# A decoder layer on one core: all mixer tiles at one pace of four steps, weights split one piece a step

## What is computed

```
x = _layernorm(x + mixer(x))            # state-space mixer over chunks of 64, 4 heads, with gate and RMS norm
x = _layernorm(x + xattn(x, ctx, ctx))  # 16 heads of 8, softmax over 256 keys
x = _layernorm(x + ffn(x))              # 8 experts, top 2 of them, 128 -> 512 -> 128, silu
```

## Time and profile before

| | |
|---|---|
| median of 3 runs | 405.66 us (405.43 to 405.94) |
| the profiled execution | 404.54 us, span 403.2 us |
| TensorE busy | 347.0 us (86%) |
| VectorE busy | 258.6 us (64%) |
| ScalarE busy | 220.2 us (55%) |
| POOL busy | 203.8 us (51%) |
| DMA | 41.97 MB, mean 104 GB/s |
| first maxima, exponentials of step 0 and of step 63 | 76.2, 107.5 and 260.1 us |

### The profile page before, as it was taken

One profiled execution on the slowest core, in us unless ns is written; L12 is line 12 of the kernel. 1 busy time (PEld: TensorE's weight loads), 2 busy tenths in 40 slices (PEclk: granted clock), 3 DMA queues, 4 the chain that ended last, 5 costly groups with the idle time before them and its releaser, 6 DMA issues.

```text
span 403.2 us, 8839 instructions
## 1 busy us (share of the span) xinstructions
PE 347.0 (86%) x2869; PEld 237.9 (59%) x2869; DVE 258.6 (64%) x794; ACT 220.2 (55%) x413; POOL 203.8 (51%) x297
## 2 busy tenths in 40 slices
PE   1999877889898999988888899989999999999900
PEld 0666654556543546454444455568878989999800
DVE  3555646788888888888888836466564444343427
ACT  2677645523476666656567776643545555555304
POOL 2760588865453535163648586535464332323425
PEclk9999999999999999999999999999999999999965
DMA  8933222545425122050723544211123211111054
GB/s 269 353 103 98 90 93 65 184 134 170 139 64 154 46 84 67 16 161 3 243 91 104 170 125 134 61 40 48 53 60 90 68 39 55 41 52 43 27 189 138
DMA packets 44461, 41.97 MB, mean 104 GB/s; under 512 B 4560, under 2 KB 38416, under 8 KB 44416
## 3 DMA queue, kind: packets, MB, share of 16 engines
q1 hardware_dynamic: 41136, 35.10, 29.0%
q0 software_dynamic: 2272, 4.69, 3.3%
q10 hardware_dynamic: 1008, 1.61, 1.1%
HBM read 26.36 MB, written 14.75 MB: 102 GB/s over the span
## 4 chain that ended last, share of the span: by engine, by line
PE 58%; DVE 18%; POOL 9%; issue 9%; ACT 4%; DMA 2%; ACTq 0%; POOLq 0%; DVEq 0%
PE banks L1028 13%; PE banks L1053 8%; DVE nm L1217 7%; PE banks L870 4%; PE banks L1043 4%; PE banks L709 4%; PE banks L918 3%; PE banks L766 2%; PE banks L774 2%; DVE ctx_in L1159 1%; PE banks L929 1%; PE banks L948 1%; PE banks L861 1%; POOL cs_wide L1616 1%; PE banks L817 1%
## 5 line engine op out<-in xcount | busy, mean ns | idle before, releaser
L1217 DVE TENSOR_REDUCE nm<-banks 128x4 f32<-128x1024 f32 x64 | 78.1, 1220 | 13.7 <-PE banks L861 12.8
L1517 ACT ACTIVATE probs_all<-banks 128x1024 f32<-128x1024 f32 x64 | 65.5, 1023 | 38.5 <-PE banks L870 38.3
L1702 POOL DMA_INDIRECT y_dram<-x,scatter_u x39 | 37.5, 962 | 55.4 <-DVE x L1364 53.1
L1028 PE MATMUL banks<-w_split,scores_in 128*128 x234 | 64.1, 409 | 0.0
L1349 DVE TENSOR_TENSOR ctx_in<-ctx_in,banks 128x512 f32<-128x512 f32 x39 | 26.8, 687 | 58.0 <-ACT ctx_in L1559 58.0
L1028 PEld LDWEIGHTS banks<-w_split,scores_in 128*128 128x128 f32 x234 | 40.8, 189 | 7.5 <-issue 0.7
L1691 POOL DMA_INDIRECT slots_dram<-rows,place_u x32 | 31.7, 991 | 25.0 <-DVE count L1309 17.6
L1559 ACT ACTIVATE ctx_in<-banks 128x512 f32<-128x512 f32 x39 | 23.3, 597 | 35.2 <-PE banks L1028 35.2
L1053 PEld LDWEIGHTS banks<-w_down,hsT 128*128 128x128 f32 x312 | 39.9, 191 | 3.2 <-issue 0.6
L1053 PE MATMUL banks<-w_down,hsT 128*128 x312 | 41.4, 276 | 0.2 <-DVE scores_in L1354 0.2
L870 PE MATMUL banks<-scores_in 32*128 32x256 f32 x256 | 32.2, 326 | 9.9 <-DVE nm L1217 5.2
(11 more groups left out here) (224 smaller groups left out, 701.4 us busy)
## 6 DMA issues: line engine op xcount, KB each, us to landing
scores_in<-k_dram SPq DMA_DIRECT2D x32, 128.0 KB, 2.6
scores_in<-q_dram SPq DMA_DIRECT2D x32, 128.0 KB, 2.7
ctx_in<-in_L_ffn_w SPq DMA_DIRECT2D x16, 256.0 KB, 3.4
cs_wide<-cs_dram SPq DMA_DIRECT2D x14, 256.0 KB, 3.6
scores_in<-slots_dram SPq DMA_DIRECT2D x39, 65.0 KB, 1.9
k_dram<-split_qk SPq DMA_DIRECT2D x8, 256.0 KB, 2.5
q_dram<-split_qk SPq DMA_DIRECT2D x8, 256.0 KB, 2.3
w_down<-in_L_ffn_wo SPq DMA_DIRECT2D x8, 256.0 KB, 3.5
```

The costliest lines, as they stand in the source:

```text
L1028: m = TE.matmul(up_bank(i, j), xT[:, i % XT, xh, :], all_up[:, c + j * FF:][:, bass.ds(expert_at[i] * UP_ALL, FF)], start=n == 0, stop=n == 2)
L1217: V.tensor_reduce(most, maxima_of(n).rearrange("p (j k q) -> p j k q", j=2, k=TPS), AX_X, ALU.max, negate=True).then_inc(s["nmax"], 1)
L1517: C.activation(probs(n).rearrange("p j k q -> p (j k q)"), EXPS, ACT.Exp, scale=SCALE).then_inc(s["probs"], 1)
L1702: G.indirect_dma_start(y_dram[:, :], bass.IndirectOffsetOnAxis(ap=scatter_u[:, i:i + 1], axis=0), y_slot[:, i % Y_RING, :], None).then_inc ...
```

## The change

Three things go together. `tile_step` becomes 4t - 33 for all tiles: tile 1 stands one step later than before, tile 7 and all behind it seven steps, and `LAST_MIXER` goes from 32 to 39. What is counted from it moves along: the second slot for maxima (from step 41), the first loads of weights (43) and the first split (45). From there on each step splits one piece, up to step 60, and every other one also loads down weights. The fillers in the mixer's bank move by three steps, so that they follow it, and `second_slot` and the wait of `scores` are written for the new parity.

```
-FIRST_TILES, FIRST_PACE, PACE = 7, 3, 4
+PACE = 4
...
-UNREAD_IN_MIX = {1: S, 4: S, 5: P, 8: 3 * P, 9: S, 13: 3 * P, 16: 3 * P, 17: 3 * P, 21: S, 24: 3 * P}
+UNREAD_IN_MIX = {4: S, 7: S, 8: P, 11: 3 * P, 12: S, 16: 3 * P, 19: 3 * P, 20: 3 * P, 24: S, 27: 3 * P}
...
 def tile_step(t):
-    return FIRST_PACE * min(t, FIRST_TILES) + PACE * max(t - FIRST_TILES, 0) - LEADS_IN
+    return PACE * t - LEADS_IN
...
-        elif n >= LAST_MIXER + 6 and piece + whole_pieces < PIECES + NE:
-            if (n - LAST_MIXER) % 3 == 2:
+        elif n >= LAST_MIXER + 6 and piece < PIECES:
+            yield "split_weights", piece
+            if W_RING <= piece + 2 < PIECES:
+                yield "load_weights", piece + 2
+            if piece % 2:
                 yield "load_down", whole_pieces
                 whole_pieces += 1
-            else:
-                yield "split_weights", piece
-                if W_RING <= piece + 2 < PIECES:
-                    yield "load_weights", piece + 2
-                piece += 1
+            piece += 1
...
         def second_slot(n):
-            return n - LEAD > LAST_MIXER and (n - LEAD - LAST_MIXER) % 2 == 1
+            return n - LEAD > LAST_MIXER and n % 2 == 0
...
-                    slots = 2 if later - LEAD > LAST_MIXER else 1
+                    slots = 2 if later - 1 - LEAD > LAST_MIXER or second_slot(later) else 1
```

## The result

| | before | changed |
|---|---|---|
| median of four runs | 405.55 us (405.40 to 405.94) | 423.54 us (420.10 to 428.35) |
| profiled execution, its span | 404.54, 403.2 us | 424.87, 423.6 us |
| mean granted clock of TensorE over the span | 0.980 | 0.921 in the profiled run, 0.911 to 0.943 in the others |

The ratio is 1.0386, with a 95% interval of 1.0332 to 1.044: slower, by 18 us between the medians where 4.9 were forecast. The ratio leaves out the run of 428.35 us, taken in a slower state, and comes to some 16 us. The time lies above the forecast's range. Where the four runs of the kernel before stay within 0.6 us of each other, those of the changed one spread over 8, and the granted clock differs along with them.

A forecast was written before the change was run, and what follows sets the result against it. It took batch 0's queries to bound the lead-in, and a nearly full TensorE the later stretches. -1.2 + 2.2 + 0.6 + 2.6 - 0.8 + 1.5 = +4.9 us on 405.66 gave 410.6 us, range 405.2 to 414.2.

The forecast's parts named there:

- rival 4: TensorE's clock falls in the gap ahead of the first maxima: +3 us, so 413.6 us; chance 0.02.
- A: Lead-in: fewer operations beside batch 0's query chain bring the first maxima earlier, -1.2 us (+0.2 to -2.5).
- D: Roots of batches 6 and 7 queue behind scatters on POOL, steps 26 and 34: +2.6 us (0.5 to 3.5).
- B: Behind the first maxima: more mixer work for TensorE and VectorE, +2.2 us (0 to 3.2).
- E: Full eight steps of attention and mixer: heavier steps spread, TensorE's gaps partly given back, -0.8 us (0 to -2.7).
- C: Second slot for maxima opens at step 41, not 33: light steps between get longer, +0.6 us (0 to 1.2).
- F: Weight loads through a ring of four places: ScalarE waits for landings at pieces 7 and 15, +1.5 us (0 to 4).
- Rival 1: Tiles, not the queries, pace the lead-in: fewer tiles save 6.8 rather than 1.2 us, 404.2 us; chance 0.10.
- Rival 2: All of the change is absorbed by gaps and TensorE's other work: +0.1 us, 405.8 us; chance 0.08.
- Rival 3: The weights' ring becomes the bound, ScalarE waits at several pieces: 5 us there, 414.1 us in all; chance 0.12.

The follow-up runs named there:

- roots_first: The changed kernel with the scatters of batches 0 and 1 behind the roots of steps 26 and 34, plus lead-in fillers: 413.85 us, ratio 1.0143.
- roots_weights: roots_first with no split of weights in steps 49 and 50: 410.98 us, ratio 1.0067 to the kernel before.
- weights_only: The kernel before with only the change's part on the weights, the mixer's pace untouched: 418.99 us, ratio 1.0016.
- lead_41: The changed kernel with a lead-in of 41 steps instead of 33 and weights split from step 37 on: 435.73 us, ratio 1.0427 to the kernel before.
- before_late_rows: The kernel before with the scatters of batch 0's rows in step 27, not 24: 422.65 us, ratio 1.0102.

## Why the prediction was wrong

The direction was right and the size was not: +4.9 forecast, +18 measured. By its own steps:

- **The step that failed is the likelihood and the price of rival 4, the fall of the clock.** I gave it 0.02 and 3 us, for one fall in the wait for the queries, directly ahead of the first maxima. In the profile TensorE has no wait there at all. The gap stood 12.5 us earlier, in the wait for x1 of batch 0, which the sum of part A doesn't have; that its 3.08 us match the 2 or 3 foreseen is luck. And the clock fell three more times, and TensorE's later stretches, where it is the bound, paid for it: 12.8 of 20.4 us between the profiles. My "some 3 us of work" took only what stands right behind the gap. A stretch of 17.1 us at 1.2 GHz cost 6.4 us and another 5.6. The Trainium skill's rule (TensorE: Matmul & The Clock Gate, section "What's actually happening") is that the gate closes after idleness and opens again after sustained work. The first half agrees with the changed kernel's trace, in that each fall came in or shortly behind waits, though of 0.8 to 3.1 us only; the second half does not, with 16.93 of 17.1 us of work at 1.2 GHz from 213.6. I had the rule and read it as a remark on one spot instead of asking it of each wait that steps A and D added.
- **A, lead-in, -1.2.** In the changed kernel the queries' last load was issued at 72.3 us, 73.0 before, with a landing of 3.1 us at most, and TensorE, at half clock up to 73.7, took them up only at 76.98. With the lead-in's fillers it does wait for the queries, 1.0 to 2.1 us, as A said, and in roots_first the first reduction came at 76.0, 0.9 before the old 76.9; in the three other runs with fillers at 77.0 to 77.6. Right in kind, but the gain was 0.9 at best; x1 of batch 0 came only 0.2 us earlier. Tile 1's gate took 0.72 for 1.67 as hoped, while the norm of two tiles still ran long (1.31 for 1.20).
- **B and E, +2.2 and -0.8.** From the first maxima to step 35, roots_weights, at full clock and without D's waits, took 121.3 us against 121.1 before. The old order's wait of 0.98 is gone in it too, so the order costs 1.2: the sum of 1.4 holds, by luck. Each part by itself does not: the steps up to step 26 gained 2.7 and those from 26 to 35 lost 3.0.
- **C, +0.6.** Steps 35 to 44 took 19.6 for 19.8. Nothing to see; that what moved there fills the light steps is my reading, not shown.
- **D, +2.6 (0.5 to 3.5).** Under-sized: 5.1 us for both waits, 4.1 above the wait that was there before. The mechanism was right; the waits (3.24 and 1.94 for 3.0 and 1.2) came out 1.0 longer together, and I took 0.6 off for other work of TensorE, of which there was none.
- **F, +1.5.** 2.0 in steps 44 to 63 of the changed order at full clock, 0.7 by the ratio of weights_only. The mechanism showed, ring and piece 7 as described, though at three pieces rather than two. The fit that the prediction takes from the Trainium skill (DMA: Bandwidth & Descriptors, section "Anatomy of one DMA — SWDGE (gpsimd) path") is for DMAs issued from GpSimd; these loads are issued from SyncE, and it is no measure of them.
- The order alone thus costs 7.6 us by the profiles (about 7 by the times) for 4.9 forecast, at 412.1 inside the forecast's own range. Of the 2.7 us between them, A makes up 1.9 (+0.7 in that run for -1.2), D 1.5 and F 0.5, and B, C and E together came out 1.2 lower than summed.
- *Rival 1* (tiles pace the lead-in) was rightly small here: a lead-in of 5 tiles instead of 6.7 saved at most 0.9 us. Its working has a slip: 4.1 us a tile is the stretch's 27.5 us over 6 2/3 tiles, while POOL's 22.4 give 3.4 a tile and a saving of 5.6, not 6.8. Whether the tiles take over once more of them stand in the lead-in, lead_41 leaves open. *Rival 2* fell. *Rival 3*: the ring cost 2, not 5; one piece waited long, not several.

## What to carry to other kernels

When a change opens waits on TensorE, price each of them twice: by its length, and by what follows if the granted clock is at half for some stretches behind it. Here 12.8 of 20.4 us were of that second kind, and they fall due in the next stretch that TensorE bounds. The fillers of such a kernel belong to one order: move the work and the places where TensorE would idle move too. And a root, a norm or any short operation queued behind a block of scatters inherits the whole block; ask for each what its consumer holds up, and when the block is moved, which root stands behind it then (before_late_rows).

## What the runs showed of the hardware

- Times that differ from run to run for one kernel went with the granted clock: the changed kernel took 417.1 us at 0.961 and 421.5 at 0.943 on one chip, 428.35 at 0.911 in the first group.
- The clock does not come back as soon as TensorE is busy again. In the stretch from 213.6 to 230.7 it worked 16.93 of 17.1 us and stayed at 1.2 GHz, and so it did for 16.02 of 17.1 from 80.5.
- Fillers ahead of a wait lower the chance of a fall; they don't exclude it. Waits of 0.8 us in light steps went before the fall at 80.5, while waits of that size left the kernel before at full clock in its profile. In one program, the changed kernel, the same wait of 1.97 us had a fall of 17.1 us behind it in one profile and none in another. Which gaps tip it, these runs don't settle.
- Chips differ. The kernel before took 405.9, 417.7 and 406.9 us on three chips with nearly the same granted clock (0.977, 0.974 and 0.977 as medians). On the slow one, in weights_only, ScalarE and VectorE sit idle at times, here while POOL scatters, though what they read was written (the maxima that VectorE reduces here had been made by 179.5), and the profile names no instruction of this core as releaser:

```profile
181.32 0.60 ACT L1492 ACTIVATE first<-banks 128x512 f32<-128x512 f32 x1 [2.50 <-remote]
...
181.44 1.23 DVE L1216 TENSOR_REDUCE nm<-banks 128x4 f32<-128x1024 f32 x1 [2.00 <-remote]
```

The traces of the other two chips have no such row, and what is behind them stays open.
